# Moving the second local layer's query, key and value stage beside the third attention, in the space of weights that are fetched again for each batch

## What is computed

```
x = x + attention(xn) * silu(ternary_ffn(xn))        # layer 0
x = x + causal_attention(xn) * silu(fp4_ffn(xn))     # layer 1
x = x + causal_attention(xn) * silu(local(xn))       # layer 2
x = x + memory(xn) * silu(experts(xn))               # layer 3
```

```
def _layer(x, wqkv, qs, ksc, wo, lg, lb, w1, b1, w2, b2):
    h = shift_token(x)
    qkv = h @ wqkv                       # 128 -> 3 * 512
    q, k, v = jnp.split(qkv, 3, axis=-1) # 8 heads of 64
    q = l2norm(q) * qs
    k = l2norm(k) * ksc
    q, k = rotary_xpos(q, k)
    o = local_attention(q, k, v)         # windows of 64, one window back
    x = x + o @ wo
    h = shift_token(x)
    h = layernorm(h) * lg + lb
    a, g = jnp.split(h @ w1 + b1, 2, axis=-1)
    x = x + (a * gelu(g)) @ w2 + b2
    return x
```

## Time and profile before

| | us |
|---|---|
| median of three runs (lowest, highest) | 4678.98 (4678.09, 4681.33) |
| time of the profiled execution | 4681.39 |
| its span, from the first to the last instruction | 4679.6 |
| PE busy in the span | 3769.4 |
| DVE busy | 2666.6 |
| ACT busy | 1891.5 |
| POOL busy | 782.5 |
| mean granted PE clock | 0.924 |

### The profile page before, as it was taken

One profiled execution on the slowest core, in us unless ns is written; L12 is line 12 of the kernel. 1 busy time (PEld: TensorE's weight loads), 2 busy tenths in 40 slices (PEclk: granted clock), 3 DMA queues, 4 the chain that ended last, 5 costly groups with the idle time before them and its releaser, 6 DMA issues. The chain is left out here.

```text
span 4679.6 us, 57461 instructions
## 1 busy us (share of the span) xinstructions
PE 3769.4 (81%) x20191; PEld 1899.0 (41%) x20355; DVE 2666.6 (57%) x5719; ACT 1891.5 (40%) x3814; POOL 782.5 (17%) x715
## 2 busy tenths in 40 slices
PE   5878888788887888887887888877888787887776
PEld 2344433435334443344433444343533444334434
DVE  5565556555566545664556555655556654566455
ACT  2443444343433434343344433444343343434324
POOL 0031101220012300222003120032101230012213
PEclk9989998999989999899998999899998999989987
DMA  4000010000000001000100001000000000100030
GB/s 139 28 8 22 5 34 28 15 14 11 28 28 28 1 18 36 20 22 1 39 28 8 22 5 34 28 9 21 11 28 28 28 1 16 36 23 22 1 81 19
DMA packets 79876, 113.86 MB, mean 24 GB/s; under 512 B 11452, under 2 KB 60167, under 8 KB 79047
## 3 DMA queue, kind: packets, MB, share of 16 engines
q1 hardware_dynamic: 73662, 101.08, 7.0%
q10 hardware_dynamic: 5898, 8.77, 0.6%
HBM read 80.68 MB, written 28.34 MB: 23 GB/s over the span
## 5 line engine op out<-in xcount | busy, mean ns | idle before, releaser
L704 DVE TENSOR_REDUCE nmax<-banks 128x1 f32<-128x512 f32 (+3 forms) x1216 | 761.1, 658 | 376.1 <-PE banks L543 208.9
L634 ACT ACTIVATE probs<-banks 128x512 f32<-128x512 f32 (+3 forms) x1536 | 673.7, 491 | 493.1 <-PE banks L561 489.9
L93 PE MATMUL banks<-filler,identb 128*128 128x512 bf16 x2384 | 689.3, 413 | 106.3 <-PEq L73 60.5
L543 PE MATMUL banks<-ks,qs 72*128 72x512 bf16 (+3 forms) x1536 | 472.0, 348 | 100.2 <-DVE nmax L704 70.2
L561 PE MATMUL banks<-qs,ks 74*128 74x512 bf16 (+3 forms) x1536 | 488.8, 352 | 39.9 <-ACT probs L634 21.5
L93 PEld LDWEIGHTS banks<-filler,identb 128*128 128x128 bf16 x2536 | 267.9, 107 | 412.2 <-issue 219.5
L599 PE MATMUL banks<-probs,v 128*32 128x512 f32 (+3 forms) x3072 | 352.9, 533 | 54.9 <-DVE att L691 33.4
L671 POOL TENSOR_SCALAR_AFFINE_SELECT probs<-probs 128x512 f32<-128x512 f32 x256 | 206.8, 809 | 1124.1 <-ACT probs L634 1124.1
L543 PEld LDWEIGHTS banks<-ks,qs 72*128 72x128 bf16 x1536 | 142.0, 101 | 427.9 <-DVE nmax L704 280.0
L333 POOL TENSOR_TENSOR rstd<-var,neghalf 128x4 f32<-128x4 f32 x24 | 24.3, 1011 | 1522.0 <-DVE var L261 1522.0
L561 PEld LDWEIGHTS banks<-qs,ks 74*128 74x128 bf16 x1536 | 144.4, 103 | 291.9 <-ACT probs L634 120.5
(11 more groups left out here) (410 smaller groups left out, 6065.8 us busy)
## 6 DMA issues: line engine op xcount, KB each, us to landing
qs<-parts_scratch SPq DMA_DIRECT2D x288, 96.0 KB
ks<-parts_scratch SPq DMA_DIRECT2D x288, 96.0 KB
parts_scratch<-parts SPq DMA_DIRECT2D x48, 384.0 KB, 2.8
qs<-max_parts SPq DMA_DIRECT2D x192, 4.0 KB
x<-in_x SPq DMA_DIRECT2D x9, 256.0 KB, 2.8
w_up_s<-in_w_up ACTq DMA_DIRECT2D x1, 2048.0 KB
x_scratch<-x SPq DMA_DIRECT2D x8, 256.0 KB, 3.7
factor_scratch<-att SPq DMA_DIRECT2D x8, 256.0 KB
```

The lines of the kernel that those rows point to most:

```text
L93: nc.tensor.matmul(K.ps[:, bank, :], K.identb[:, :], K.filler[:, :], start=True, stop=True)
L543: mm = nc.tensor.matmul(K.ps[:, b, i * keys:(i + 1) * keys], K.qs[0:72, 4 * g + j, t * P:(t + 1) * P], K.ks[0:72, 4 * g + j, 0:keys], star ...
L634: nc.scalar.activation(probs[:, 4 * (q % QUADS) + m % 4, q0:T], K.ps[:, bank("second", m), q0:T], ACT.Exp, scale=scale).then_inc(exped, 1)
L704: nc.vector.tensor_reduce(nmax[:, t, h:h + len(heads)], K.ps[:, n % 2, 0:len(heads) * keys].rearrange("p (j k) -> p j k", k=keys), AX.X, A ...
```

## The change

The stage `local_qkv(.., 1)` as a block of its own is gone. A new class `GluThenQkv` runs the first `Glu` beside the third attention as before, and then, from step 13 on, turns and shifts its result and makes queries, keys and values of the second local layer. Table `TILE_STEPS` says at which step each of the ten pieces of each of the four tiles is issued: tile 0 from step 16 to 28, tile 1 from 29, tile 2 from 34, tile 3 from 39 to 48. `KEEPS_BUSY = False` takes out the constant matmuls from step 34 on in this attention alone. The root and reciprocal of the norms (ACT and DVE) become one power on POOL. The banks for a tile are the pair 6 and 7, and for tile 2 the pair 0 and 1 once the first scores are over.

Queries, keys and values need space that lives on into `local_attention`. It is that of the five ternary matrices, now one tile `shared` of 22 KB in each partition (`late_qT`, `late_kT`, three tiles of `late_v`), and `xnT` for the fourth tile of values. `experts` therefore fetches the five matrices again in every batch, behind its load of the next `x`, and waits for them at its end. POOL's masks and the pieces of the `Beside` are now issued in the order of the steps.

```
@@ attention, on POOL
             def _(pool):
-                beside.run(beside.on_gpsimd)
                 if causal:
                     for q in range(4 * NG):
                         k = q % NT
+                        beside.run(beside.on_gpsimd, LAG + 2 * q)
                         pool.wait_ge(exped, 4 * (q + 1))
...
+                beside.run(beside.on_gpsimd)
@@ attention, on PE
-                            if causal and s > 8 * NG + 1:
+                            if causal and s > 8 * NG + 1 and beside.KEEPS_BUSY:
                                 keep_busy(nc, K, 0, 1)
@@ new
+class GluThenQkv(Glu):
+    KEEPS_BUSY = False
+    Y_STEP = 13
+    BANKS = ((6, 7), (6, 7), (0, 1), (6, 7))
+    TILE_STEPS = ((16, 17, 18, 20, 22, 24, 25, 26, 27, 28), tuple(range(29, 39)), tuple(range(34, 44)),
+                  tuple(range(39, 49)))
...
+    def gpsimd(self, pool):
+        yield from super().gpsimd(pool)
+        nc, K = self.nc, self.K
+        for step, t, i in self.steps(2, 4, 5, 6):
+            yield step
+            if i == 2:
+                pool.wait_ge(self.clipped, 2 * t + 2)
+                if t >= 2:
+                    pool.wait_ge(self.q_scaled, t - 1)
+                nc.gpsimd.tensor_tensor(self.rn[:, t % 2, :, :].rearrange("p m h -> p (m h)"),
+                                        self.ssq[:, t % 2, :, :].rearrange("p m h -> p (m h)"), K.neghalf[:, 0:2 * LH],
+                                        ALU.pow).then_inc(self.rn_done, 1)
+            elif i == 6:
+                pool.wait_ge(self.rn_done, t + 1)
+                pool.wait_ge(self.added, 2 * t + 2)
+                x = self.qk[t % 2][1].rearrange("p (h d) -> p h d", d=LD)
+                nc.gpsimd.tensor_tensor(x, x, self.rn[:, t % 2, 1, :].unsqueeze(2).to_broadcast([P, LH, LD]),
+                                        ALU.mult).then_inc(self.k_scaled, 1)
+            else:
+                m = i - 4
+                pool.wait_ge(self.rotated, 2 * t + m + 1)
+                x = self.qk[t % 2][m]
+                nc.gpsimd.tensor_tensor(x, x, self.rot[m], ALU.add).then_inc(self.added, 1)
@@ experts, on SP
                 sp.dma_start(K.x[:, :, :], next_x).then_inc(loaded, 16)
+                for dst, src in K.w0_loads:
+                    sp.dma_start(dst, src).then_inc(reloaded, 16)
...
                 sp.wait_ge(loaded, 16)
+                sp.wait_ge(reloaded, 16 * len(K.w0_loads))
@@ batch_loop
+    shared = sb("shared", [P, 11 * T])
+    K.w0_h1, K.w0_h2 = [shared[:, 4 * T * i:4 * T * (i + 1)].rearrange("p (k n) -> p k n", n=T) for i in range(2)]
...
+    K.late_qT, K.late_kT = K.w0_h1, K.w0_h2
+    late_v = [shared[:, (8 + t) * T:(9 + t) * T] for t in range(NT - 1)]
...
-                attention(nc, K, True, K.w2_ao, K.b2_ao, combine=False, beside=Glu(nc, K, both, 0, False))
-            local_sublayer(nc, K, 1)
+                attention(nc, K, True, K.w2_ao, K.b2_ao, combine=False, beside=GluThenQkv(nc, K, both))
+            with ExitStack() as tmp:
+                K.qT, K.kT, K.v_tm = K.late_qT, K.late_kT, K.late_v
+                K.oT = sbuf(nc, tmp, "oT2", [P, LH // 2, T])
+                local_attention(nc, K, 1)
```

More of the change, by code:

```diff
@@ L432 @@
     BEFORE = 0
+    KEEPS_BUSY = True
     started = False
@@ L494, in attention @@
     beside = beside or Beside()
+    beside.first_read, beside.first_uses = reduced, PER * NG
     if not beside.started:
@@ L1020, in scalar @@
                 nc.scalar.activation(sq[:, m, :], K.ps[:, b + m, :], ACT.Square).then_inc(squared, 1)
-            nc.scalar.activation(K.v_tm[:, t, :], K.ps[:, b + 2, :], ACT.Identity).then_inc(v_copied, 1)
+            nc.scalar.activation(K.v_tm[t], K.ps[:, b + 2, :], ACT.Identity).then_inc(v_copied, 1)
             act.wait_ge(clipped, t + 1)
@@ L1270, in __init__ @@
          self.gelu_done, self.hid_ready, self.down, self.yturned, self.shifted) = K.pool[24:37]
+        self.y_ready = K.pool[37]
         self.y_bank, self.back_bank, self.turn_bank, self.down_bank = (7, 0, 1, 6) if alone else (7, 6, 7, 6)
@@ L1349, in vector @@
         nc.vector.tensor_tensor(K.y[:, :, :], K.y[:, :, :],
-                                K.b2_down[L][:, :].unsqueeze(1).to_broadcast([P, NT, D]), ALU.add)
+                                K.b2_down[L][:, :].unsqueeze(1).to_broadcast([P, NT, D]),
+                                ALU.add).then_inc(self.y_ready, 1)
     def gpsimd(self, pool):
@@ L1376, in local_buffers @@
 def local_buffers(nc, K, ctx):
-    K.v_tm = sbuf(nc, ctx, "v_tm", [P, NT, INNER])
+    v_tm = sbuf(nc, ctx, "v_tm", [P, NT, INNER])
+    K.v_tm = [v_tm[:, t, :] for t in range(NT)]
     K.qT = sbuf(nc, ctx, "qT", [P, LH // 2, T])
@@ L1419, in experts @@
      stored, loaded) = K.pool[0:24]
+    reloaded = K.pool[24]
     th = slice(64, 96)
@@ L1700, in batch_loop @@
     K.b0_qkv = whole("b0_qkv", bc=True, loads=soon)
-    K.w0_1, K.w0_2, K.w0_h1, K.w0_h2, K.w0_3 = [
-        whole(n, loads=soon) for n in ("w0_1", "w0_2", "w0_h1", "w0_h2", "w0_3")]
+    shared = sb("shared", [P, 11 * T])
+    K.w0_h1, K.w0_h2 = [shared[:, 4 * T * i:4 * T * (i + 1)].rearrange("p (k n) -> p k n", n=T) for i in range(2)]
+    K.w0_1, K.w0_2 = shared[:, 8 * T:9 * T], shared[:, 9 * T:10 * T]
+    K.w0_3 = shared[:, 10 * T:11 * T].rearrange("p (k n) -> p k n", n=D)
+    K.w0_loads = [(K.w0_1, A["w0_1"][:, :]), (K.w0_2, A["w0_2"][:, :])] + [
+        (t, A[n][:, :, :]) for t, n in ((K.w0_h1, "w0_h1"), (K.w0_h2, "w0_h2"), (K.w0_3, "w0_3"))]
+    soon.extend(K.w0_loads)
+    K.late_qT, K.late_kT = K.w0_h1, K.w0_h2
+    late_v = [shared[:, (8 + t) * T:(9 + t) * T] for t in range(NT - 1)]
     K.s0_1, K.s0_2, K.s0_h1, K.s0_h2 = [whole(n, loads=soon) for n in ("s0_1", "s0_2", "s0_h1", "s0_h2")]
@@ L1739, in batch_loop @@
     K.xnT = sb("xnT", [P, T])
+    K.late_v = late_v + [K.xnT[:, :]]
     K.identb = sb("identb", [P, P], BF16)
```

143 lines of the change are left out of this document (122 added, 21 removed).

## The result

| | us |
|---|---|
| median of four runs (lowest, highest) | 4616.32 (4610.85, 4620.16) |
| kernel before, same chip | 4679.01 (4678.09, 4681.33) |
| ratio, 95% interval | 0.9863 (0.9848 to 0.9877) |
| span of the profiled run | 4614.6 |

The change makes the kernel 1.4% faster, by 63 us. I had forecast 154, and the time lies above my range. The page after answers to the earlier trace rows: PE has 61 us less to do, POOL 91 more.

A forecast was written before the change was run, and what follows sets the result against it. PE was taken as nearly full in steps 13 to 32, with room on the engines in 33 to 49. Saving 33.4 less growth 14 gave 19.4 us a batch, 155 in eight: 4525 us, range 4474 to 4592.

The forecast's parts named there:

- What goes: The separate stage between third attention and local attention goes, less a remaining barrier: 33.4 us saved in a batch.
- The constants, 4.3 us off PE: Third attention's tail: taking out 20 constant matmuls at 0.21 us each relieves PE of 4.3 us.
- rival (b): Without constants, waits between matmul groups lower PE's clock in the tail: growth 24 us, time 4606; chance 0.07.
- The power, 2.0 us: POOL's power for a tile's norms, size 128x16: guessed 2.0 us, between 1.0 and 3.5.
- Steps 13 to 32, 7 us: Third attention's first part, nearly full on PE: new pieces lengthen it by 7 us, least 4, most 10.
- Steps 33 to 49, 7 us, at most 12: Third attention's tail: 19.5 us of work plus some 5 of gaps, growth 7 us, least 3.5, most 12.
- The fetch at nothing: Fetching the ternary matrices again in `experts` is hidden and costs nothing; 8 us in a batch without that cover.
- Contention, 0.14 each on POOL: POOL's operations meeting DVE's cost 0.14 us each, 1.1 us of POOL in a batch, included in the sum.
- rival (a): POOL bounds the tail, power going by element and queued masks holding PE: growth 18 to 24, time 4575; chance 0.20.
- Rival (e): The moved work doesn't overlap and costs the attention what it cost alone, 30 us: time 4654; chance 0.04.

The follow-up runs named there:

- the best version: Changed kernel with values' matmul of tiles 1 to 3 one step later, ten constants at step 44, and tile 0's power one step later on POOL: 4583.8 us.
- e1_mult: Changed kernel with POOL's power replaced by a multiplication of the same operands (wrong norms in the second local layer): 4562.6 us, ratio 0.9751 to the kernel before.

## Why the prediction was wrong

- **What goes**: right. 33.4 us forecast; 35.6 us before against 2.0 after, so 33.6.
- **The constants, 4.3 us off PE**: wrong as a gain. Taken out of the kernel before they cost 40 us, and put back into the changed kernel they made PE's work 3.5 us longer and the time no different. Their price on PE is not the path's. The rule that I weighed under rival (b) was the better guide, and I set it aside for a row with 2.8 of 5 us and a clock of 1.00.
- **The power, 2.0 us**: measured 2.91, inside its bounds.
- **Steps 13 to 32, 7 us**: measured 9.8, inside its bounds. In the two batches where the clock holds at 0.97 it is 8.0; in the other six the clock is 0.92 or 0.93, and the first part 1 to 3 us longer than in those two.
- **Steps 33 to 49, 7 us, at most 12**: measured 13.6. This is the step that failed, in the words "with some 5 us of such gaps over the 19.5 the part takes 24.3". The part takes 30.8 us: PE works 21.7 where I had 19.5, in part at the lower clock, and waits 9.1 where I had some 5. The gaps were a guess, and they are the larger error. 6.4 us of them lie ahead of the last weighing. In the second batch PE waits there 1.6 us for DVE's maxima, twice 1.1 for POOL's masks, and 0.8 and 0.6 for the tiles' pieces on DVE. The others are at the end, where I had the output follow almost at once behind the last quad: it stands 2.9 us behind the last tile's turned queries. This end is where the power counts: with 0.22 us for it, and also with POOL's load put back off the chain, the tail is 28.2 and 28.4 us. The order of the last tile's transposes and the output's was not tried the other way round, so what that wait is worth by itself is not shown.
- **The fetch at nothing**: right, by the run without it.
- **Contention, 0.14 each on POOL**: mostly on the other side. POOL's additions take 1.32 us in the mean, less than the 1.41 in the sum, but DVE's scalings of queries take 1.25 in the mean where they take 0.69 alone, and 1.67 when they begin within POOL's addition; I had that price on POOL only.
- **Left out**: 2.0 us in a batch in other blocks, 1.7 of them in `experts`, by PE's clock.
- **A slip**: by the prediction's own sum rival (a)'s least growth of 18 us gives 4558 us, and not 4548. Nothing hangs on it.

In sum 19.4 us in a batch were forecast and 8.1 came (the span's 65.0 over eight). The 11.3 missing: 2.8 in the first part, 6.6 in the tail, 2.0 elsewhere. Rival (a) had a growth of 18 to 24 and a time up to 4606; the growth was 23.4, so its size was nearly right, and its mechanism only in part: the power is worth 5.2 us of it, and taking load off POOL didn't make the kernel faster. Rival (b) was real too, with a share that the runs don't separate: the best version regains 4.0 us in a batch, by its clock and by its order on PE and POOL. Rival (e) is far off: without overlap the time is 4791, not 4654. The time lies 24 us above the range: three misses, all to the same side, added up. What stays open is why the part ahead of the last weighing takes the 5.0 us more of waits that it does, piece by piece, why `experts` starts at the lower clock in more batches, and how much of the tail would be left at a full clock throughout; with the constants at step 44 it is 29.5 us in those at 1.00.

## What to carry to other kernels

Where work with a long chain is laid in pieces beside other work, an engine sum is a floor only: follow the pieces through each queue, with their waits. See what the block's own output stands behind at the end, and follow the last piece's chain to there. Look at what stands behind each new wait in an in-order queue, above all behind a piece whose input comes late, and put ready work ahead of it; but a fixed order that puts waiting work ahead of a chain's links costs more. Constants on PE are to be judged by running the kernel with and without them: in this kernel before the change their going cost 40 us, and in the changed kernel it cost nothing.

## What the runs showed of the hardware

- POOL's power takes 1.02 us on 128x4 and 2.91 on 128x16, and a multiplication of 128x16 takes 0.22.
- Logarithm and exponential, one behind the other, load ACT's tables twice, 1.28 us each.
- DVE's scaling of 128x512 takes 0.68 to 0.69 us alone and 1.67 when POOL's addition began 0.14 us ahead of it; where both began at once (in `e1_mult`) DVE took 0.69 and POOL's addition 1.82 in place of 1.27. In these rows one of them is held back, for most of the length that they share.
- The clock of a stretch isn't the same in all batches of one execution, though the instructions and their waits are: behind a wait of PE of 1.35 us it fell in six of eight batches and held in two.
- Twenty short constant matmuls in each batch of the kernel before, taken out, cost 40 us in the eight. The clock of its tails fell from 1.00 to between 0.62 and 0.81, with no wait of PE longer than 0.97 us.
